# Query and key transposes of a two-layer attention and mixture kernel by transposing DMAs, a third bank for the first score pass, and the batch's work in a new order

## The reference, cut to what matters

```
q = (x @ Wq.T + bq).reshape(B, L, H, hd)      # B=8, L=256, H=16, hd=8
k = (x @ Wk.T + bk).reshape(B, L, H, hd)
v = (x @ Wv.T + bv).reshape(B, L, H, hd)
q, k = _apply_rope(q, cos, sin), _apply_rope(k, cos, sin)   # first attention only
scores = jnp.einsum('bqhd,bkhd->bhqk', q, k) / np.sqrt(hd)
attn = jax.nn.softmax(scores, axis=-1)
out = jnp.einsum('bhqk,bkhd->bqhd', attn, v).reshape(B, L, D)
```

## Time and profile before

| what | value |
| --- | --- |
| median of 3 runs | 602.04 us (600.29 to 603.62) |
| profiled execution, its own time | 603.38 us |
| its span, first to last instruction | 601.6 us |
| PE, DVE, ACT, POOL busy | 538.7, 429.6, 413.9, 344.2 us |
| mean granted TensorE clock | 0.939 of full |
| DMA | 43.12 MB, mean 72 GB/s |

### The profile page before, as it was taken

One profiled execution on the slowest core, in us unless ns is written; L12 is line 12 of the kernel. 1 busy time (PEld: TensorE's weight loads), 2 busy tenths in 40 slices (PEclk: granted clock), 3 DMA queues, 4 the chain that ended last, 5 costly groups with the idle time before them and its releaser, 6 DMA issues.

```text
span 601.6 us, 16720 instructions
## 1 busy us (share of the span) xinstructions
PE 538.7 (90%) x5262; PEld 388.6 (65%) x5262; DVE 429.6 (71%) x1582; ACT 413.9 (69%) x1104; POOL 344.2 (57%) x471
## 2 busy tenths in 40 slices
PE   9899999999779984799999999979999999999950
PEld 7444444447557973544555444758889999999940
DVE  4979999966765304877989996786887788643276
ACT  2279998882624752538999988417778888999824
POOL 4978888342005782673445544456566777777730
PEclk9979999998999997958999999779999999999975
DMA  7493000002001237007910000112221122111363
GB/s 215 112 322 101 2 1 3 2 2 71 7 1 43 47 40 223 6 1 218 302 46 2 3 2 1 54 39 58 51 52 54 59 62 61 59 58 55 125 186 120
DMA packets 53204, 43.12 MB, mean 72 GB/s; under 512 B 14992, under 2 KB 43424, under 8 KB 52992
## 3 DMA queue, kind: packets, MB, share of 16 engines
q1 hardware_dynamic: 45568, 29.98, 17.3%
q0 software_dynamic: 7264, 11.62, 7.4%
q10 hardware_dynamic: 288, 0.46, 0.2%
HBM read 30.17 MB, written 11.87 MB: 70 GB/s over the span
## 4 chain that ended last, share of the span: by engine, by line
PE 70%; DVE 12%; issue 6%; DMA 5%; ACT 4%; POOL 2%; DVEq 0%; ACTq 0%; POOLq 0%; SPq 0%
PE bank L1329 12%; PE bank L1339 11%; PE bank L928 10%; PE bank L911 7%; PE bank L893 6%; PE bank L945 3%; ACT prob L1477 2%; DMA parts<-augs,idx_s 2%; PE bank L969 2%; DVE W L1965 2%; PE bank L1141 2%; PE bank L1382 1%; PE bank L1161 1%; PE bank L953 1%; PE bank L1200 1%
## 5 line engine op out<-in xcount | busy, mean ns | idle before, releaser
L1792 DVE TENSOR_REDUCE mx<-bank 128x2 f32<-128x512 f32 x256 | 163.1, 686 | 24.7 <-PE bank L893 23.7
L1477 ACT ACTIVATE prob<-bank 128x512 f32<-128x512 f32 x256 | 140.7, 609 | 23.0 <-PE bank L911 19.1
L1666 ACT ACTIVATE queries<-bank,prob 128x128 f32<-128x128 f32 x316 | 90.4, 369 | 19.9 <-PE bank L1329 17.0
L1329 PE MATMUL bank<-keys,prob 128*128 x632 | 85.7, 278 | 0.8 <-issue 0.6
L1339 PE MATMUL bank<-W,queries 128*128 x632 | 84.2, 276 | 0.0
L804 POOL DMA_INDIRECT prob<-xs,idx_g x64 | 61.8, 966 | 33.7 <-DVE idx_g L2176 12.6
L1329 PEld LDWEIGHTS bank<-keys,prob 128*128 128x128 f32 x632 | 76.8, 192 | 3.9 <-issue 2.6
L893 PE MATMUL bank<-keys,queries 32*128 32x256 f16 x512 | 77.0, 285 | 2.6 <-issue 1.7
L1339 PEld LDWEIGHTS bank<-W,queries 128*128 128x128 f32 x632 | 76.7, 192 | 1.8 <-issue 0.7
L928 PE MATMUL bank<-prob,augs 128*32 128x256 f32 x1024 | 77.7, 392 | 0.0
L813 POOL DMA_INDIRECT parts<-augs,idx_s x64 | 63.4, 991 | 21.5 <-issue 9.0
(11 more groups left out here) (292 smaller groups left out, 1045.3 us busy)
## 6 DMA issues: line engine op xcount, KB each, us to landing
W<-in_w SPq DMA_DIRECT2D x48, 256.0 KB, 4.0
sum<-zero SPq DMA_DIRECT2D x3, 1024.0 KB, 9.1
xs<-X SPq DMA_DIRECT2D x2, 768.0 KB, 5.2
prob<-xs,idx_g POOLq DMA_INDIRECT x80, 2.6
XB<-sum SPq DMA_DIRECT2D x1, 1024.0 KB, 4.9
Y<-sum SPq DMA_DIRECT2D x4, 256.0 KB, 5.7
W<-sum SPq DMA_DIRECT2D x4, 256.0 KB, 6.5
parts<-augs,idx_s POOLq DMA_INDIRECT x64, 2.2
```

What stands on the lines that cost most here:

```text
L1329: last = nc.tensor.matmul(bank[2 + p % 2][:, P * f:P * f + P], wc[:, p % 4, P * f:P * f + P], xsT2[:, bass.ds(at, 1), :], start=True, stop ...
L1477: nc.scalar.activation(prob[:, v % 8, :, :], st_bank(b, v)[:, :], ACT.Exp, scale=SCALE).then_inc(exp_done, 1)
L1666: last = nc.scalar.activation(hid2[:, p % 4, f, :], bank[2 + p % 2][:, P * f:P * f + P], ACT.Gelu, bias=wc[:, p % 4, WB + f:WB + f + 1])
L1792: nc.vector.tensor_reduce(m_at, bank[S1B[u % 2]][:, :].rearrange("p (j k) -> p j k", j=2), AX.X, ALU.max).then_inc(s1_used, 1)
```

## The change

From batch 1 of each layer on, `query_transposes`, `key_transposes`, `q_evac` and `keys_evac` are gone. SP issues two transposing DMAs for each batch instead (`turn`), one for each half of the rows, from `aug` to `qkT`, a buffer of three slots that holds queries and keys; they wait for `aug_ready` (now raised twice for a batch), and for the reads of the slot's old content. PE's unit 0 waits for both DMAs (`turned_in`). Batch 0 of each layer is still turned by PE. POOL builds `aug` ahead of `vaug`. The s1 units go round over the banks 0, 1 and 6. `pe_iteration` has a new order, and the expert loads, the constants and the clears are issued between the transposing DMAs of the batches.

```
-        S1B, STB, OTB, M5, M6, M7 = (0, 1), (2, 3), 4, 5, 6, 7
+        S1B, STB, OTB, M5, M6, M7 = (0, 1, 6), (2, 3), 4, 5, 6, 7
...
-                last = engine.tensor_tensor(A[:, t, H:2 * H, HD:2 * HD], s4[:, t, H:2 * H, :],
-                                               A[:, t, H:2 * H, 0:HD], ALU.subtract)
-            last.then_inc(aug_ready, 1)
+                engine.tensor_tensor(A[:, t, H:2 * H, HD:2 * HD], s4[:, t, H:2 * H, :],
+                                     A[:, t, H:2 * H, 0:HD], ALU.subtract).then_inc(aug_ready, 1)
...
+            def turn(lay, b):
+
+                g = b + NB * lay
+                if b > 2:
+                    sp.wait_ge(st_done, 16 * (g - 2))
+                wait_for(sp, turned_in, 32 * (g - 1 - lay))
+                for t in range(2):
+                    sp.wait_ge(aug_ready, 2 * g + t + 1)
+                    sp.dma_start_transpose(qkT[b % 3][:, t, :, :], aug[b % 2][:, t, :, :].rearrange("p h x -> p (h x)")
+                                           ).then_inc(turned_in, 16)
+
+            def batches_in(lay):
+
+                at = ((0, 0, 4, 8, 8, 8, 8, 8), (0, 0, 3, 6, 9, 12, 15, 16))[lay]
+                for b in range(1, NB):
+                    turn(lay, b)
+                    if lay == 0 and b == 1:
+                        constants_in()
+                    if lay == 1 and b == 2:
+                        sp.wait_ge(join_xt, 4)
+                    for e in range(at[b - 1], at[b]):
+                        expert_weights(lay, e)
+                    if lay == 0 and b == 4:
+                        sums_zeroed()
...
-                build_vaug(lay, i, par)
                 if i < NB - 1:
                     build_aug(pool, lay, i + 1, 1 - par)
+                build_vaug(lay, i, par)
...
+                if i > 0 and u == 0:
+                    pe.wait_ge(turned_in, 32 * (g - lay))
+                if i == 0 and u == 2:
+                    pe.wait_ge(kt_ready, 2 * lay + 2)
+                if g > 0 or u > 2:
+                    pe.wait_ge(s1_used, 16 * g + u - 2)
...
                     if u == 5 and tail_on:
                         bt(lay, i - 2, 1)
-                    if u in (7, 9) and soft_on:
-                        av(lay, i - 1, nxt, 0, u // 9)
+                    if u == 7 and soft_on:
+                        st(lay, i - 1, nxt, 4)
+                        st(lay, i - 1, nxt, 5)
+                        av(lay, i - 1, nxt, 0, 0)
...
-                    if u == 13 and front_on:
-                        query_transposes(lay, i + 1, nxt)
-                    if u == 15 and tail_on:
-                        out_product(lay, i - 2)
-                    if u == 15 and front_on:
-                        key_transposes(lay, i + 1, nxt)
...
-                    if u == 13 and front_on:
-                        q_evac(lay, i + 1, nxt)
-                    if u == 15 and tail_on:
+                    if u == 13 and tail_on:
                         output_added(lay, i - 2)
```

More of the change, by code:

```diff
@@ L270, in program @@
         proj_done = sem("proj_done")
+        turned_in = sem("turned_in")
         qkv_ready = sem("qkv_ready")
@@ L885, in s1 @@
                 rows = slice(HP * q, HP * q + HP)
-                if u == 0:
-                    pe.wait_ge(tq_ready, g + 1)
-                if u in (0, 4):
-                    pe.wait_ge(kt_ready, 2 * g + u // 4 + 1)
-                if not (isinstance(i, int) and g == 0 and u < 2):
-                    pe.wait_ge(s1_used, 16 * g + u - 1)
+                if i == 0 and u == 0:
+                    pe.wait_ge(tq_ready, lay + 1)
+                if i == 0 and u in (0, 4):
+                    pe.wait_ge(kt_ready, 2 * lay + u // 4 + 1)
+                if i > 0 and u == 0:
[4 more added lines that the diff above has]
+                    pe.wait_ge(s1_used, 16 * g + u - 2)
                 for j in range(2):
-                    last = nc.tensor.matmul(bank[S1B[u % 2]][:, L * j:L * j + L], QT[par][rows, 2 * jp + j, P * qt:P * qt + P],
-                                            keyT[par][rows, 2 * jp + j, :], start=True, stop=True)
+                    last = nc.tensor.matmul(bank[S1B[(16 * i + u) % 3]][:, L * j:L * j + L], qkT[i % 3][rows, qt, 2 * jp + j, :],
+                                            qkT[i % 3][rows, :, NJ + 2 * jp + j, :], start=True, stop=True)
                 last.then_inc(s1_done, 1)
@@ L1155, in query_transposes @@
                 g = b + NB * lay
-                pe.wait_ge(aug_ready, g + 1)
-                if not (isinstance(b, int) and b in (0, NB - 1)):
-                    pe.wait_ge(qkv_ready, 2 * g + 4)
+                pe.wait_ge(aug_ready, 2 * g + 2)
                 for j in range(NJ):
                     for t in range(2):
-                        last = nc.tensor.transpose(half[M5][:, L * j + P * t:L * j + P * t + P],
+                        last = nc.tensor.transpose(half[M5][:, P * (4 * t + j):P * (4 * t + j) + P],
                                                    aug[par][:, t, 4 * j:4 * j + 4, :], ident_h[:, :])
@@ L1166, in key_transposes @@
                 g = b + NB * lay
-                pe.wait_ge(aug_ready, g + 1)
-                if not (isinstance(b, int) and b == 0):
-                    pe.wait_ge(kt_ready, 2 * g)
+                pe.wait_ge(aug_ready, 2 * g + 2)
                 for j in range(NJ):
                     for t in range(2):
-                        last = nc.tensor.transpose(half[M6][:, L * j + P * t:L * j + P * t + P],
+                        last = nc.tensor.transpose(half[M6][:, P * (4 * t + j):P * (4 * t + j) + P],
                                                    aug[par][:, t, H + 4 * j:H + 4 * j + 4, :], ident_h[:, :])
```

143 lines of the change are left out of this document (73 added, 70 removed).

## The result

The changed kernel takes 625.43 us (median of 4 runs, 622.37 to 628.25), the kernel before in the same session 602.83 us (4 runs, 600.29 to 607.03). The ratio is 1.0367, 95% interval 1.0289 to 1.0444: 22.6 us slower, where I had forecast 15 us faster and a range that ended at 612. The profiled execution took 625.64 us, its span is 623.8 us, its mean granted clock 0.920.

The account below looks back on a forecast made before the run. DVE's work plus its waits for PE (12.93 + 1.31 us) was taken to set a batch. Gains of 15.9 less 1.0 for DMAs took 603.38 to 588.5, or 587 against 602.04; forecast 583 to 591, wider range 580 to 612.

Parts of the forecast that it names:

- POOL's order: On POOL, building `aug` ahead of `vaug` readies `aug` about 1.2 us earlier; only `av`, an iteration later, waits behind `vaug`.
- Third bank and new order: On PE and DVE: nearly covers 1.28 us without an s1 unit, taking DVE's waits from 1.31 to 0.65 us.
- Rival A: In the attentions: only the copy of the queries counts, DVE's waits stay; batch 13.6 us, time 594.5 us; chance 0.20.
- The copy of the queries: Goes from DVE in iterations 0 to 6 of both layers, saving 14 x 0.61 = 8.5 us.
- The transposing DMAs: On SP's queue: 4.0 to 5 us to landing, hidden; 0.5 us may show in batch 1 of each layer.
- E: Time from maxima ready (L1808) of batch k until both transposing DMAs landed for batch k+2; up to 12.9 us free.
- SP's queue: Expert loads between turns finish about 18 us after L1808, DMAs due at 19.6; hidden with 1 to 2 us spare.
- Rivals B and C: Transposing DMAs: B, show in part, 590 to 603 us, chance 0.12; C, set batch, 7 us per us of E, 0.20.
- The far bound: For one transposing DMA: result written in 8192 runs of 32 bytes, 36.5 ns each over 16 engines, 18.7 us.
- rival D: PE, with fewer transposes, idles and its clock falls in middle batches: 13 to 18 us, time 600 to 605; chance 0.04.

Follow-up runs that it names:

- experiment 6: Idle matmuls ahead of unit 0 of batches 1 and 7, in the changed kernel with three `vraw` buffers, then (second kernel) with two: ratios 0.9841 and 1.0258.
- the repaired kernel: The changed kernel with three `vraw` buffers instead of two, all else kept: ratios 0.9848 and 0.9834 against the kernel before.
- the fastest version: Changed kernel with three `vraw` buffers, old order of PE, ACT and DVE, and idle matmuls ahead of batch 1: 589.91 against 602.62 us, ratio 0.9795.

## Why the prediction was wrong

**The step that failed** is in "POOL's order": "Behind `vaug` waits only `av` of the same batch, which comes an iteration later." ACT's copy in `front_evac` waits for it too, for the `vraw` buffer, in the same iteration. I had read POOL's timeline only for what the swap brings forward and not asked of the step that goes back what else waits for it; the sum has no term for it. The line of code was there, `act.wait_ge(vaug_ready, g - 1)`; the view of waits did not show it, because in the trace of before `vaug` was always early. The price is the changed kernel against the same with a third buffer: 220.0 against 190.6 to 195.7 in the attention sum, 24 to 29 us. On 602 us the ratios make it 31 to 32 us, and the differences within each session 33 to 34 (22.6 slower, 10.6 and 11.0 faster). The part of it that goes beyond the windows I have not located.

**Third bank and new order** was mis-sized. I gave the waits of DVE 0.65 us of a middle batch, and 12.97 and 13.05 in all. Measured with the wait lifted, 13.35 with 12.22 of DVE busy, so 1.13 of waits, and 14.19 with 12.41, so 1.78. In eight middle batches this is 4 x 0.38 + 4 x 1.14 = 6.1 us, which is the distance between my 587 and the 592.6 to 593.4 that ratios of 0.9834 and 0.9848 make of 602.6. Rival A, which left the waits as they were, had 594.5: without the failed step it would have been the nearest. The reason that I gave for the gain (0.83 of idle, a third bank covers it) held for 0.25 to 0.48 us in layer 0; the order that I thought harmless gave some back in layer 1.

**The copy of the queries** was right: DVE's busy time in a middle batch went from 12.93 to 12.22 with a third `vraw` and 12.33 as changed, against 0.61 forecast.

**The transposing DMAs** were hidden in the middle batches with more to spare than I forecast, and not hidden at both ends of layer 0. In a middle batch of the changed kernel the second one is issued at 69.7 and lands 2.8 us later, E of 10.8 us (forecast 11.3 to 12.3, free up to 12.9). Ahead of batch 7 it was issued at 123.4 and took 4.7 us to land, at about 128.0, E of 12.7:
```profile
128.06 0.51 PE L912 MATMUL bank<-keys 32*128 32x256 f16 x4 [0.77 <-DMA keys<-augs]
```
My 12.9 was the length of a middle batch; batch 6 is only 12.47 long, so unit 0 waited 0.77 us, the clock fell (mean 0.88), and batch 7 took 14.51 us where I had 12.6. The same batch is 12.78 and 14.49 in the two runs with three `vraw` buffers. Why this DMA lands late I have not found; from 126 on the DMA engines were busy 3% of the time or less. At batch 1 of layer 0 they cost more than my 0.5: besides the wait, 2.6 to 2.8 us by the clock in the new order (experiment 6). SP's queue hid its loads: no middle batch of the repaired kernel waits for a DMA. Rivals B and C fall for the changed kernel as the cause of its loss: its list of waits has 2.8 us for them, two times. The far bound of 18.7 us a DMA fell as well; it had 8192 runs where the trace has 1056 packets. 1309 ns for a block ("VectorE: DVE Perf Modes" of the Trainium skill, "The three transpose paths"), which that page gives for one 128x128 transpose and not as a price for each of several, would make an estimate of 10.5 us of the eight blocks of one DMA if it added up. It does not; the trace has this, issue and landing:
```profile
L605 SPq DMA_TRANSPOSE keys<-augs x28: 1232/1307/2307, 21.6 to 373.1; - x28
...
DMA to landing us min/median/max: 2.7/2.8/4.7
```
**The clock** (rival D) fell in the middle batches, to 0.82 and 0.90, but as a consequence: with the wait lifted it is 1.00 in the same batches.

**What stays open.** The gain of the fastest version is 12.7 us, of which 7.7 lie in the windows; the other 5 lie ahead of, between and behind them and I did not follow them. The stretches between and behind scatter by themselves: among four kernels with the same mixtures and no gain to show (before twice, before with three `vraw` buffers, the DMAs alone) they are 141.4 to 144.3 and 232.1 to 235.9 us. That batch 1 is 15.4 in one and 17.4 us in the other of two equal kernels is mostly the landing of its second DMA, 3.5 and 5.2 us after the issue; why that differs is open.

## What to carry to other kernels

When a step is moved back in an engine's list, search the code for every wait on the semaphore that it raises, and for each ask how much slack it has; the trace of before shows no wait that was always met. An engine's idle time says nothing on whether the step could run in it; its own waits do. A buffer of two slots ties the reader of batch i to the writer of batch i+2: moving the reader needs a third slot or a check of that pair. And a part that looks bad in a bundle may be the one that the others need: here POOL's swap costs 5% alone and 3% as shipped, and with one buffer more it is worth 1.5 to 2.3%, by the ratios of three pairs of kernels over several sessions.

## What the runs showed of the hardware

One transposing DMA of 256 KB from 128 partitions to 128 holds SP's queue for 1.31 us (median), three times the 0.43 us of a plain issue, and lands 2.8 us after its issue in the median, faster than the 4.0 of an expert load, though single ones took up to 4.7 in the changed kernel and 5.2 in the one with three `vraw` buffers. It has 1056 packets by the difference of the two q1 rows, (75136 - 45568) / 28, and these took (22.9% of 623.8 - 17.3% of 601.6) x 16 us / 29568 = 21 ns each by this estimate, less than the 36.5 ns that I had worked with; so about 1.4 us of all 16 engines for a DMA. What mattered was not this but the time from the second half's readiness to its landing: 3.4 us in a middle batch (10.8 less 7.4), of which 0.6 are the wait for the issue of the first, and 5.3 us ahead of batch 7.

An idle PE can pay twice. After stretches with 0.51 and 0.55 us of PE in 2 us, and with none in 2 us, the granted clock stood at 0.50 for some us of full work; waits of 1.4 and 3.0 us in batch 1 cost 2.6 to 2.8 us more in this way, and one of 0.77 us ahead of batch 7 was followed by a clock of 0.60 in the next 1 us. It is not a matter of the long gap alone: in the second kernel of experiment 6 the mean clock was 1.00, 0.83 and 0.50 in three stretches of 2 us in a row (from 28 to 34) in which PE was busy 1.71, 1.66 and 2.00 us.
